# Sum of the experts' outputs: the second norm's scale and shift move from Pool to VectorE, in another order

## The chip, the cores and the metric

One NeuronCore of one Trainium2 chip runs the whole program, and the metric is the device time of one execution in microseconds. It has TensorE (PE), VectorE (DVE), ScalarE (ACT), GpSimd (POOL, here called Pool) and SyncE (SP), each with its own queue of instructions, which it works through in order.

## What is computed

Four blocks follow each other on x of 2 x 2048 x 256 (4096 rows of 256): agent attention, attention with a mixture of experts (MoE), a selective scan, and a feed-forward block with FP4 rounding. Each is wrapped as `x = x + layernorm(block(layernorm(x)))`. The change lies at the end of the second block, where the experts' outputs come together:

```python
    out = jnp.einsum('ne,end->nd', w, y)          # y = h @ W2 + b2, w: the two best gates
    ...
    x = _ln(src + attn_out, ln1_g, ln1_b)
    ff = _moe(x, gW, gb, W1, b1, W2, b2)
    return _ln(x + ff, ln2_g, ln2_b)
...
x = x + _layernorm(_L0_ffn_ref(_layernorm(x, axis=-1), ...), axis=-1)
x = x + _layernorm(_L1_attn_ref(_layernorm(x, axis=-1), ...), axis=-1)
```

`_L1_attn_ref` begins with a norm of its own with `w_norm` and `b_norm`.

## The kernel before, in words

`build` (end of the file) calls the stages one after another. Each stage opens its own buffers and semaphores and ends with a barrier of all engines. The change is in `moe_output`, which runs between `experts` and `scan_inputs`.

`moe_output` works on 8 groups (`GROUPS`) of 512 rows, each as 4 tiles (`GT`) of 128 rows by 256 channels. Every large buffer has two slots, for even and odd groups. For a group g the work goes like this:

- **Pool** gathers the two experts' output rows of every token from DRAM, by index, with eight indirect DMAs (`gather`, line 1661) into `back`.
- **TensorE** adds it all up in PSUM, in `ps_b[slot]` (`bias`, lines 1729 to 1733): b2 by gates, the row x of the norm before, and the two gathered rows. The text calls this pass g. `turn_gates` (line 1718) turns the gates for it, and ScalarE copies them (`copy_gate_t`, line 1670).
- **VectorE** takes the statistics of ps_b (`stats_y`, line 1605), and **ScalarE** norms it into y (`norm_y`, line 145).
- **Pool** multiplies y by ln2_g (line 1650) and adds ln2_b, giving v (line 1654), in `scale_y`. That is the second norm.
- VectorE takes the statistics of v (`stats_v`), ScalarE norms v in place (`norm_v`), VectorE adds x1 (`add_x1`, line 1632) giving x2 and takes its statistics; ScalarE norms x2 into xm (`norm_x2`), VectorE takes its statistics (`stats_xm`), ScalarE norms xm into xn (`norm_xm`), TensorE turns xn (`turn_xn`, line 1741), and ScalarE scales and shifts the turned xn and stores it (`scale_xn`, line 1703). SP loads x1 and stores x2 and xm.

So there are four norms in a row. The order of each engine's queue is written out by `run_stages`: in step s it issues every stage `(stage, behind)` for group s - behind, in the order of the list. With `unroll=True` all steps stand one after another. The arithmetic of all four norms' scales is done once a step for four groups at a time, each at another norm: `all_scales` on VectorE (lines 98 to 107, then, after ScalarE's line 113 and 115, lines 134 to 140). There are 11 such steps (`STEPS`, 0 to 10). In the text, step s begins on VectorE where line 98 of `all_scales(s)` starts.

The lists of the kernel before:

```python
dve:  (stats_y, 0), (stats_v, 1), (all_scales, 0, STEPS), (add_x1, 1), (stats_xm, 2)
pool: (gather, -2), (scale_y, 0)
act:  (copy_gate_t, -1), (all_rstd, 0, STEPS), (norm_y, 0), (norm_v, 1), (norm_x2, 2), (norm_xm, 3), (scale_xn, 4)
pe:   (turn_gates, -1), (bias, -1), (turn_xn, 4)
sp:   (load_x1, 0), (store_x2, 1), (store_xm, 2)
```

Waits that matter around the change: `gather(g)` waits for pass g-2 (`bias_ready`), whose rows lie in the same slot; pass g waits for its gathers, its copied gates and `norm_y(g-2)`; `scale_y(g)` waits for all four tiles of y; `add_x1(g)` waits for `norm_v(g)`, which ScalarE does in step g+1. Pool's queue starts with a wait for `loaded`, the five small loads that SP issues at the stage's start (b2, ln2_g, ln2_b, w_norm, b_norm), lines 1572 to 1577.

Of the kernel before, what the change touches and what calls it, by code (L numbers as in the profile page):

```python
# [16 lines left out]
ALU = mybir.AluOpType  # L17
# [3 lines left out]
P = 128  # L21
B, L, C = 2, 2048, 256
# [3 lines left out]
GT = 4  # L26
GN = GT * P
GROUPS = T // GN
# [102 lines left out]
def ln_scale(dve, chain, s, n, rstd_ready, scale_ready):  # L131

    dve.wait_ge(rstd_ready, n + 1)
    chain.then(dve.tensor_tensor(s.t[:, 0, :], s.r0[:, :], s.r0[:, :], ALU.mult))
    chain.wait()
    chain.then(dve.scalar_tensor_tensor(s.t[:, 0, :], s.t[:, 0, :], -0.5, s.var[:, :], ALU.mult, ALU.mult))
    chain.wait()
    chain.then(dve.scalar_tensor_tensor(s.rstd[:, :], s.t[:, 0, :], 1.5, s.r0[:, :], ALU.add, ALU.mult))
    chain.wait()
    dve.scalar_tensor_tensor(s.nmr[:, :], s.mean[:, :], -1.0, s.rstd[:, :], ALU.mult, ALU.mult).then_inc(scale_ready, 1)  # L140
# [12 lines left out]
def run_stages(eng, units, *stages, unroll=False, ways=2):  # L153

    stages = [(stage, behind, own[0] if own else units) for stage, behind, *own in stages]

    def step(s, way):
        for stage, behind, count in stages:  # L160
            if not isinstance(s, int) or 0 <= s - behind < count:
                stage(s - behind, (way - behind) % ways)

    starts, ends = [behind for _, behind, _ in stages], [behind + count for _, behind, count in stages]
    if unroll:
        for s in range(min(starts), max(ends)):
            step(s, s % ways)
        return

    first, last = -(-max(starts) // ways) * ways, min(ends) // ways * ways  # L170
    for s in range(min(starts), first):
        step(s, s % ways)
    with eng.Fori(first // ways, last // ways) as i:
        for way in range(ways):
            step(i * ways + way, way)
    for s in range(last, max(ends)):
        step(s, s % ways)


def third_on(unit):  # L180

    return not isinstance(unit, int) or unit >= 2
# [6 lines left out]
def over(ap, shape):  # L189

    return ap.broadcast_to(shape)
# [484 lines left out]
STEPS = NQ * QC  # L676
# [862 lines left out]
def moe_output(nc, io, scratch, route, sent, ident):  # L1539
# [3 lines left out]
    with ExitStack() as ctx:  # L1543
        r = Room(nc, ctx, "mo")
        NORMS = 4
        STEPS = GROUPS + NORMS - 1
        b2 = r.sb("b2", [E, C])
        rows = {n: r.sb(n, [P, 1, C]) for n in ("ln2_g", "ln2_b")}
# [4 lines left out]
        x1, y, v, x2, xm, xn = (r.sb(n, [P, 2, GT, C]) for n in ("x1", "y", "v", "x2", "xm", "xn"))  # L1553
# [5 lines left out]
        loaded = r.sem("loaded")  # L1559
# [4 lines left out]
        y_normed, y_scaled, v_ready, v_normed = (r.sem(n) for n in ("y_normed", "y_scaled", "v_ready", "v_normed"))  # L1564
        x2_ready, xm_ready, xn_normed = (r.sem(n) for n in ("x2_ready", "xm_ready", "xn_normed"))
# [3 lines left out]
        with nc.Block() as block:  # L1569
            @block.sync  # L1570
            def _(sp):
                sp.dma_start(b2[:, :], io["b2"]).then_inc(loaded, 16)
                for n, dst in rows.items():
                    sp.dma_start(dst[:, 0, :], over(io[n], [P, C])).then_inc(loaded, 16)
                with nc.allow_non_contiguous_dma("scale and shift by channel"):
                    for n, dst in columns.items():
                        sp.dma_start(dst[:, :], io[n].rearrange("o (k p) -> p (o k)", p=P)).then_inc(loaded, 16)

                def load_x1(g, slot):
                    if third_on(g):  # L1580
                        sp.wait_ge(x2_ready, g - 1)
                    sp.dma_start(x1[:, slot, :, :], rows_at(scratch.x1, g * GN)).then_inc(x1_loaded[slot], 16)

                def store_x2(g, slot):
                    sp.wait_ge(x2_ready, g + 1)
                    sp.dma_start(rows_at(scratch.x2, g * GN), x2[:, slot, :, :]).then_inc(x2_stored[slot], 16)

                def store_xm(g, slot):
                    sp.wait_ge(xm_ready, (g + 1) * GT)
                    sp.dma_start(rows_at(scratch.xm, g * GN), xm[:, slot, :, :]).then_inc(xm_stored[slot], 16)  # L1590

                for slot in range(2):

                    for s in (x2_stored, xm_stored, xn_t_stored):
                        sp.sem_inc(s[slot], 16)
                run_stages(sp, GROUPS, (load_x1, 0), (store_x2, 1), (store_xm, 2))
                for slot in range(2):
                    for s in (x2_stored, xm_stored, xn_t_stored):
                        sp.wait_ge(s[slot], (GROUPS // 2 + 1) * 16)

            @block.vector
            def _(dve):
                def stats(n, x):
                    for k in range(GT):
                        dve.bn_stats(ln.st[:, n * GT + k, :], x[:, k, :]).then_inc(stats_ready[n], 1)

                def stats_y(g, slot):
                    dve.wait_ge(bias_ready, g + 1)
                    stats(0, ps_b[slot])

                def stats_v(g, slot):
                    dve.wait_ge(v_ready, g + 1)
                    stats(1, v[:, slot, :, :])

                def all_scales(s, parity):
                    for n in range(NORMS):
                        if 0 <= s - n < GROUPS:
                            dve.wait_ge(stats_ready[n], (s - n + 1) * GT)
                    if s >= NORMS:
                        dve.wait_ge(xn_normed, (s - NORMS + 1) * GT)  # L1620
                    c = Chain(dve, steps, s * (VAR_STEPS + SCALE_STEPS))
                    ln_var(dve, c, ln, var_ready)
                    ln_scale(dve, c, ln, s, rstd_ready, scale_ready)
                    assert c.n == VAR_STEPS + SCALE_STEPS, c.n

                def add_x1(g, slot):
                    dve.wait_ge(x1_loaded[slot], (g // 2 + 1) * 16)
                    dve.wait_ge(x2_stored[slot], (g // 2 + 1) * 16)
                    dve.wait_ge(v_normed, (g + 1) * GT)
                    if g >= 2:  # L1630
                        dve.wait_ge(xm_ready, (g - 1) * GT)
                    dve.tensor_tensor(x2[:, slot, :, :], v[:, slot, :, :], x1[:, slot, :, :], ALU.add).then_inc(x2_ready, 1)
                    dve.wait_ge(x2_ready, g + 1)
                    stats(2, x2[:, slot, :, :])

                def stats_xm(g, slot):
                    dve.wait_ge(xm_ready, (g + 1) * GT)
                    stats(3, xm[:, slot, :, :])

                dve.memset(ln.st[:, :, :], 0.0).then_inc(stats_zeroed, 1)  # L1640
                dve.wait_ge(stats_zeroed, 1)
                run_stages(dve, GROUPS, (stats_y, 0), (stats_v, 1), (all_scales, 0, STEPS), (add_x1, 1), (stats_xm, 2), unroll=True)

            @block.gpsimd
            def _(pool):
                pool.wait_ge(loaded, 5 * 16)

                def scale_y(g, slot):
                    pool.wait_ge(y_normed, (g + 1) * GT)
                    pool.tensor_tensor(y[:, slot, :, :], y[:, slot, :, :], over(rows["ln2_g"][:, :, :], [P, GT, C]), ALU.mult).then_inc(y_scaled, 1)  # L1650
                    if third_on(g):
                        pool.wait_ge(x2_ready, g - 1)
                    pool.wait_ge(y_scaled, g + 1)
                    pool.tensor_tensor(v[:, slot, :, :], y[:, slot, :, :], over(rows["ln2_b"][:, :, :], [P, GT, C]), ALU.add).then_inc(v_ready, 1)

                def gather(g, slot):
                    if third_on(g):
                        pool.wait_ge(bias_ready, g - 1)
                    for a in range(2):
                        for t in range(GT):  # L1660
                            pool.indirect_dma_start(back[:, slot, a, t, :], None, scratch.sorted_y[:, :],  # L1661
                                                    bass.IndirectOffsetOnAxis(route.packed[:, a, g * GT + t:g * GT + t + 1], 0)).then_inc(gathered[slot], 16)

                run_stages(pool, GROUPS, (gather, -2), (scale_y, 0), unroll=True)

            @block.scalar
            def _(act):
# [1282 lines left out]
```

## Time and profile before

| | |
|---|---|
| median of 3 runs | 3812.51 us (3805.7 to 3818.8) |
| the profiled execution's own time | 3818.61 us |
| its span, first to last instruction | 3816.9 us |
| busy over the span | PE 86%, DVE 77%, ACT 54%, POOL 31% |
| mean granted clock of TensorE | 0.915 |
| stage `moe_output` in the span | 2146 to 2335 us |

The profile is of one execution, with times from the span's start. A row of the timeline is: start in us, length in us, engine, line, operation, output<-inputs, shape, count, and in brackets the idle time of that engine just before and what ended it. "issue" is time in which an engine waited for nothing that the profile shows. PEclk is the share of full speed that TensorE's clock was granted. PEld is TensorE's weight load.

### The profile page before, as it was taken

What the parts mean: (1) busy time and instruction counts of PE and PEld (TensorE: products, weight loads), DVE (VectorE), ACT (ScalarE), POOL (GpSimd) and SP (SyncE); (2) the same over time, 40 slices, a digit from 0 to 9 for tenths busy, and PEclk for the clock granted to TensorE, in tenths of its full rate; (3) what the DMA queues carried; (4) which work ended last, traced back from release to release, by engine and by line L of the source; (5) the groups of instructions that cost most, each with busy time, mean ns of one, the idle gap of its engine ahead of it and who ended that gap; (6) DMA issues with size and microseconds to landing.
All of it is one profiled execution on the core that took longest, in us unless ns stands there. A gap on an engine that the chain in (4) does not pass through costs nothing. (4 is left out here: it accounts for less than half of the span.)

```text
span 3816.9 us, 87664 instructions
## 1 busy us (share of the span) xinstructions
PE 3298.5 (86%) x34938; PEld 1884.3 (49%) x34939; DVE 2927.6 (77%) x4552; ACT 2057.6 (54%) x2972; POOL 1173.3 (31%) x910
## 2 busy tenths in 40 slices
PE   4769999999999999968699775997799999747876
PEld 1433333333333333326466552343687787546665
DVE  5659999998999999706344254676699999868986
ACT  0316777776777777833011155665565766334553
POOL 0100000000000000005100270000799999747775
PEclk8868999998999999967899866998899999879998
DMA  1674023030303120043222253333543434211110
GB/s 55 220 187 47 13 42 46 8 48 6 48 4 49 20 34 5 5 154 118 79 65 64 75 160 117 112 124 133 138 132 116 133 116 134 90 57 50 55 33 17
DMA packets 221875, 296.93 MB, mean 78 GB/s; under 512 B 56377, under 2 KB 154946, under 8 KB 219842
## 3 DMA queue, kind: packets, MB, share of 16 engines
q1 hardware_dynamic: 204258, 258.24, 25.1%
q0 software_dynamic: 6144, 17.05, 1.4%
q10 hardware_dynamic: 11120, 16.62, 1.3%
q8 instruction: 260, 4.26, 0.5%
q14 instruction: 93, 0.76, 0.1%
HBM read 174.75 MB, written 116.47 MB: 76 GB/s over the span
## 5 line engine op out<-in xcount | busy, mean ns | idle before, releaser
L921 DVE TENSOR_REDUCE att_maxima<-att_ps_m 128x1 f32<-128x512 f32 x2048 | 1286.4, 684 | 90.8 <-PE att_ps_m L977 89.3
L876 ACT ACTIVATE att_probs<-att_ps_s 128x1024 f32<-128x1024 f32 x1024 | 1000.0, 1022 | 289.9 <-PE att_ps_o L1004 276.7
L1004 PE MATMUL att_ps_o<-att_probs,att_vs 128*32 128x256 f32 x8192 | 662.6, 396 | 4.8 <-ACT att_probs L876 0.6
L977 PE MATMUL att_ps_m<-att_ks,att_qs 48*128 48x512 f32 x2048 | 587.3, 515 | 29.3 <-DMA att_ks<-scratch_k 28.6
L2235 POOL TENSOR_TENSOR ss_ch<-ss_h,ss_c_rep 128x1024 f32<-128x1024 f32 x256 | 601.6, 2416 | 12.4 <-DVE ss_h L2322 12.4
L2354 PE MATMUL ss_ps_u<-ss_diag,ss_dx_t 128*32 128x128 f32 x16384 | 476.0, 275 | 28.1 <-DMA ss_dx_t<-scratch_dx_t 14.6
L2354 PEld LDWEIGHTS ss_ps_u<-ss_diag,ss_dx_t 128*32 128x32 f32 x16384 | 454.2, 111 | 84.8 <-issue 63.9
L977 PEld LDWEIGHTS att_ps_m<-att_ks,att_qs 48*128 48x128 f32 x2048 | 238.7, 189 | 477.0 <-DVE att_maxima L921 393.6
L992 PE MATMUL att_ps_s<-att_qs,att_ks 50*128 50x512 f32 x2048 | 456.7, 407 | 4.0 <-DMA att_qs<-att_m_parts 1.2
L2274 ACT ACTIVATE ss_decay<-ss_delta,ss_a_neg 128x1024 f32<-128x1024 f32 x256 | 293.9, 1148 | 232.1 <-DVE ss_h L2322 210.1
L1004 PEld LDWEIGHTS att_ps_o<-att_probs,att_vs 128*32 128x32 f32 x8192 | 163.0, 108 | 365.1 <-issue 342.3
L2322 DVE TENSOR_TENSOR_SCAN ss_h<-ss_decay,ss_ps_u 128x1024 f32<-128x1024 f32 x128 | 286.4, 2275 | 47.5 <-PE ss_ps_u L2354 38.3
L2322 DVE TENSOR_TENSOR_SCAN ss_h<-ss_decay,ss_carry,ss_ps_u 128x1024 f32<-128x1024 f32 x128 | 293.2, 2334 | 7.7 <-POOL ss_ch L2235 4.8
L992 PEld LDWEIGHTS att_ps_s<-att_qs,att_ks 50*128 50x128 f32 x2048 | 223.4, 190 | 25.0 <-ACT att_probs L876 20.8
L856 POOL TENSOR_TENSOR att_heads<-att_o_t,att_sums 128x256 f32<-128x256 f32 x32 | 19.9, 621 | 702.0 <-DVE att_sums L936 702.0
L849 POOL TENSOR_TENSOR att_m_parts<-att_m_t,att_m_parts 16x128 fp32r<-16x128 f32 x32 | 14.4, 449 | 682.8 <-ACT att_m_parts L896 682.8
L1457 ACT ACTIVATE ex_y<-ex_ps_y,ex_x 128x256 f32<-128x256 f32 x72 | 34.1, 474 | 301.7 <-PE ex_ps_y L1528 301.7
L1661 POOL DMA_INDIRECT mo_back<-scratch_sorted_y,moe_packed x64 | 61.2, 956 | 345.5 <-DMA mo_b_norm<-in_b_norm 318.8
L2036 PE MATMUL si_ps_xz<-si_xn_t,si_w_in 128*128 128x512 f32 x256 | 119.4, 622 | 35.1 <-ACT si_xp L1984 15.8
L2375 PE MATMUL ss_ps_y<-ss_ch,ss_sum_block 128*32 128x512 f32 x1024 | 124.7, 602 | 15.3 <-POOL ss_ch L2235 15.1
L1510 PE MATMUL ex_ps_h<-moe_w_w,ex_x_t 128*128 x288 | 137.2, 599 | 0.4 <-issue 0.4
L1528 PE MATMUL ex_ps_y<-moe_w_w,ex_hid_t 128*128 x576 | 136.1, 379 | 0.0
(391 smaller groups left out, 4472.6 us busy)
## 6 DMA issues: line engine op xcount, KB each, us to landing
ss_delta<-scratch_delta SPq DMA_DIRECT2D x256, 128.0 KB, 3.1
att_qs<-scratch_q SPq DMA_DIRECT2D x96, 128.0 KB, 9.3
att_ks<-scratch_k SPq DMA_DIRECT2D x96, 128.0 KB, 10.7
ex_x<-scratch_sorted_x SPq DMA_DIRECT2D x72, 132.0 KB, 2.1
scratch_sorted_y<-ex_y SPq DMA_DIRECT2D x72, 128.0 KB, 1.7
scratch_v<-qkv_v_ext SPq DMA_DIRECT2D x8, 1024.0 KB, 4.4
scratch_q<-qkv_parts SPq DMA_DIRECT2D x16, 512.0 KB, 5.3
scratch_k<-qkv_parts SPq DMA_DIRECT2D x16, 512.0 KB, 6.0
```

The source lines that it names most:

```text
L876: act.activation(probs[:, (2 * n + pair) % 4, :, :], ps_s[pair][:, :, :], ACT.Exp, scale=HD ** -0.5).then_inc(exp_done, 1)
L921: dve.tensor_reduce(maxima[:, j, at:at + 1], ps_m[plan.bank(key)][:, :], AX.X, ALU.max).then_inc(maxed, 1)
L977: pe.matmul(ps_m[plan.bank(key)][:, :], qs[own, s // QC % 2, s % QC, p, t * P:(t + 1) * P], ks[own, s // QC % 2, p, c * GN:(c + 1) * GN], ...
L992: mm = pe.matmul(ps_s[pair][:, e, :], ks[rows_of(e, 0, ROWS), st // QC % 2, pair, kt * P:(kt + 1) * P], qs[rows_of(e, 0, ROWS), st // QC % ...
L1004: mm = pe.matmul(ps_o[h * VW:(h + 1) * VW, cols], vs[st // QC % 2][:, kt, h * VW:(h + 1) * VW], probs[:, (2 * n + h // 2) % 4, h % 2, cols ...
L1510: mm = pe.matmul(ps_h[slot][:, :], x_t[:, slot, k, :], w1[:, bass.ds(e, 1), k, :].rearrange("p a f -> p (a f)"), start=k == 0, stop=k == K ...
L1528: mm = pe.matmul(ps_y[slot][:, 0, :], hid_t[:, slot, f, :], w2[:, bass.ds(e, 1), f, :].rearrange("p a c -> p (a c)"), start=f == 0, stop=f ...
L2235: pool.tensor_tensor(ch[:, w.n % (CH_GROUPS * DQ), :], h[:, w.n % H_SLOTS, :], c_rep[:, w.ng, :], ALU.mult).then_inc(s["ch_ready"], 1)
L2274: act.activation(decay[:, w.n % DECAYS, :], delta[:, w.delta % DELTAS, :], ACT.Exp, scale=a_neg[:, at:at + 1]).then_inc(s["decay_ready"], 1)
L2322: dve.tensor_tensor_scan(h[:, w.n % H_SLOTS, :], decay[:, w.n % DECAYS, :], ps_u[w.n % U_BANKS][:, :], start, ALU.mult, ALU.add).then_inc( ...
L2354: mm = pe.matmul(ps_u[w.n % U_BANKS][q * DSUB:(q + 1) * DSUB, j * P:(j + 1) * P], dx_t[:, w.part % 2, j, w.dq * DSUB:(w.dq + 1) * DSUB], d ...
L2375: mm = pe.matmul(ps_y[dq * DSUB:(dq + 1) * DSUB, cols], block[:, :], ch[:, group % CH_GROUPS * DQ + dq, cols], start=False, stop=group % N ...
```

## The change

VectorE gets `scale_y`, with both operations as they were on Pool, and the wait for the five loads. Its list gets a new order, in which `all_scales` comes first in a step and `stats_y` works for the next group. Pool keeps only `gather`, with no wait for the loads and no waits for VectorE. The wait for x2 inside `scale_y` is dropped, since VectorE itself makes x2. The other engines' lists stay.

```diff
+                def scale_y(g, slot):
+                    dve.wait_ge(y_normed, (g + 1) * GT)
+                    dve.tensor_tensor(y[:, slot, :, :], y[:, slot, :, :], over(rows["ln2_g"][:, :, :], [P, GT, C]), ALU.mult).then_inc(y_scaled, 1)
+                    dve.wait_ge(y_scaled, g + 1)
+                    dve.tensor_tensor(v[:, slot, :, :], y[:, slot, :, :], over(rows["ln2_b"][:, :, :], [P, GT, C]), ALU.add).then_inc(v_ready, 1)
...
-                run_stages(dve, GROUPS, (stats_y, 0), (stats_v, 1), (all_scales, 0, STEPS), (add_x1, 1), (stats_xm, 2), unroll=True)
+                dve.wait_ge(loaded, 5 * 16)
+                run_stages(dve, GROUPS, (all_scales, 0, STEPS), (stats_y, -1), (scale_y, 0), (add_x1, 1), (stats_v, 0), (stats_xm, 2), unroll=True)
...
-                pool.wait_ge(loaded, 5 * 16)
-
-                def scale_y(g, slot):
-                    pool.wait_ge(y_normed, (g + 1) * GT)
-                    pool.tensor_tensor(y[:, slot, :, :], y[:, slot, :, :], over(rows["ln2_g"][:, :, :], [P, GT, C]), ALU.mult).then_inc(y_scaled, 1)
-                    if third_on(g):
-                        pool.wait_ge(x2_ready, g - 1)
-                    pool.wait_ge(y_scaled, g + 1)
-                    pool.tensor_tensor(v[:, slot, :, :], y[:, slot, :, :], over(rows["ln2_b"][:, :, :], [P, GT, C]), ALU.add).then_inc(v_ready, 1)
...
-                run_stages(pool, GROUPS, (gather, -2), (scale_y, 0), unroll=True)
+                run_stages(pool, GROUPS, (gather, -2), unroll=True)
```

VectorE, the end of step 2 of `moe_output` (from the last line of `all_scales(2)` to the first of `all_scales(3)`), as a difference. The names: mo_ps_b is the sum in PSUM, mo_x the buffers x1, x2, mo_ln_g and mo_ln_b the rows ln2_g and ln2_b.

```order
 L140 SCALAR_TENSOR_TENSOR mo_ln_nmr<-mo_ln_mean,mo_ln_rstd 128x16
-L1632 TENSOR_TENSOR mo_x<-mo_v,mo_x 128x1024
+L1605 BN_STATS mo_ln_stats<-mo_ps_b 128x6 x4
+L1613 TENSOR_TENSOR mo_y<-mo_y,mo_ln_g 128x1024
+L1615 TENSOR_TENSOR mo_v<-mo_y,mo_ln_b 128x1024
+L1638 TENSOR_TENSOR mo_x<-mo_v,mo_x 128x1024
 L1605 BN_STATS mo_ln_stats<-mo_x 128x6 x4
+L1605 BN_STATS mo_ln_stats<-mo_v 128x6 x4
 L1605 BN_STATS mo_ln_stats<-mo_xm 128x6 x4
-L1605 BN_STATS mo_ln_stats<-mo_ps_b 128x6 x4
-L1605 BN_STATS mo_ln_stats<-mo_v 128x6 x4
 L98 TENSOR_TENSOR mo_ln_t<-mo_ln_stats 128x16
```

The statistics of the next sum moved from the end of the step to right behind the arithmetic, ahead of the two operations that are new on VectorE and of the addition of x1.

Pool, the start of the stage before:

```order
L1644 UNCONDITIONAL_BRANCH
L1661 DMA mo_back<-scratch_sorted_y,moe_packed 128x256 x24
L1650 TENSOR_TENSOR mo_y<-mo_y,mo_ln_g 128x1024
L1654 TENSOR_TENSOR mo_v<-mo_y,mo_ln_b 128x1024
L1661 DMA mo_back<-scratch_sorted_y,moe_packed 128x256 x8
L1650 TENSOR_TENSOR mo_y<-mo_y,mo_ln_g 128x1024
```

And Pool's whole stage now:

```order
L1124 UNCONDITIONAL_BRANCH
L59 ISA x2
L1651 UNCONDITIONAL_BRANCH
L1658 DMA mo_back<-scratch_sorted_y,moe_packed 128x256 x64
L1569 UNCONDITIONAL_BRANCH
L59 ISA
```

The 64 gathers follow each other with nothing between them but their own waits for the passes.

## Rows read from the trace of the kernel before

**Rows 1.** Windows: busy us of each engine (instructions), PEclk, DMA share, GB/s.
```profile
2146.00:2335.00 189.00, 117.39 (x416) 78.29 (x416) 79.53 (x258) 83.08 (x174) 102.81 (x80) 0.64 0.43 135
...
2163.00:2179.00 16.00, 16.00 (x42) 10.26 (x43) 0.00 (x0) 0.00 (x0) 6.20 (x7) 0.50 0.23 66
...
2225.20:2233.60 8.40, 8.40 (x40) 5.73 (x41) 3.49 (x17) 4.94 (x12) 6.46 (x7) 1.00 0.36 103
2237.40:2247.40 10.00, 9.97 (x40) 6.86 (x41) 6.88 (x27) 2.72 (x7) 8.03 (x8) 0.83 0.71 225
2255.40:2271.30 15.90, 15.87 (x40) 10.33 (x41) 10.82 (x29) 8.25 (x18) 12.93 (x10) 0.50 0.67 209
```

**Rows 2.** Timeline of VectorE in the stage.
```profile
2146.21 0.14 DVE L1640 MEMSET mo_ln_stats<- 128x96 f32 x1 [6.50 <-PEq L60]
...
2180.52 0.19 DVE L98 TENSOR_TENSOR mo_ln_t<-mo_ln_stats 128x16 f32<-128x16 f32 x1
...
2201.76 1.23 DVE L1632 TENSOR_TENSOR mo_x<-mo_v,mo_x 128x1024 f32<-128x1024 f32 x1 [4.05 <-ACT mo_v L145]
...
2226.61 0.19 DVE L98 TENSOR_TENSOR mo_ln_t<-mo_ln_stats 128x16 f32<-128x16 f32 x1
...
2242.71 0.19 DVE L98 TENSOR_TENSOR mo_ln_t<-mo_ln_stats 128x16 f32<-128x16 f32 x1
...
2244.90 0.17 DVE L140 SCALAR_TENSOR_TENSOR mo_ln_nmr<-mo_ln_mean,mo_ln_rstd 128x16 f32<-128x16 f32 x1
2249.19 3.64 DVE L1632 TENSOR_TENSOR mo_x<-mo_v,mo_x 128x1024 f32<-128x1024 f32 x1 [4.12 <-ACT mo_v L145]
2252.86 1.41 DVE L1605 BATCH_NORM_STATS2 mo_ln_stats<-mo_x 128x6 f32<-128x256 f32 x4
2254.19 1.39 DVE L1605 BATCH_NORM_STATS2 mo_ln_stats<-mo_xm 128x6 f32<-128x256 f32 x4
...
2294.12 0.19 DVE L98 TENSOR_TENSOR mo_ln_t<-mo_ln_stats 128x16 f32<-128x16 f32 x1
...
2305.98 0.19 DVE L98 TENSOR_TENSOR mo_ln_t<-mo_ln_stats 128x16 f32<-128x16 f32 x1
```

**Rows 3.** Timeline of Pool in the stage.
```profile
2151.24 1.00 POOL L1661 DMA_INDIRECT mo_back<-scratch_sorted_y,moe_packed  x1 [318.79 <-DMA mo_b_norm<-in_b_norm]
...
2202.70 1.10 POOL L1661 DMA_INDIRECT mo_back<-scratch_sorted_y,moe_packed  x1 [0.30 <-issue]
...
2249.39 2.35 POOL L1650 TENSOR_TENSOR mo_y<-mo_y,mo_ln_g 128x1024 f32<-128x1024 f32 x1
2251.88 3.15 POOL L1654 TENSOR_TENSOR mo_v<-mo_y,mo_ln_b 128x1024 f32<-128x1024 f32 x1
```

**Rows 4.** Groups of Pool in the stage: busy us, mean ns, idle before.
```profile
L1661 POOL DMA_INDIRECT mo_back<-scratch_sorted_y,moe_packed x64 | 61.2, 956 | 345.5 <-DMA mo_b_norm<-in_b_norm 318.8 <-issue 17.5 <-PE mo_ps_b L1733 8.7
L1654 POOL TENSOR_TENSOR mo_v<-mo_y,mo_ln_b 128x1024 f32<-128x1024 f32 x8 | 22.8, 2848 | 1.0
L1650 POOL TENSOR_TENSOR mo_y<-mo_y,mo_ln_g 128x1024 f32<-128x1024 f32 x8 | 18.8, 2352 | 22.3 <-ACT mo_y L145 22.2
```

**Rows 5.** Timeline of TensorE: first matmuls of passes 1, 3, 6 and 7.
```profile
2180.48 0.69 PE L1729 MATMUL mo_ps_b<-mo_b,mo_gate_t 8*128 8x256 f32 x2 [0.68 <-ACT mo_gate_t L1670]
...
2207.68 1.19 PE L1729 MATMUL mo_ps_b<-mo_b,mo_gate_t 8*128 8x256 f32 x2 [7.80 <-DMA mo_back<-scratch_sorted_y,moe_packed]
...
2255.43 1.22 PE L1729 MATMUL mo_ps_b<-mo_b,mo_gate_t 8*128 8x256 f32 x2 [6.51 <-ACT mo_gate_t L1670]
...
2275.30 1.09 PE L1729 MATMUL mo_ps_b<-mo_b,mo_gate_t 8*128 8x256 f32 x2 [2.14 <-ACT mo_gate_t L1670]
```

**Rows 6.** Timeline of ScalarE: a full step, its first and last row.
```profile
2245.11 1.94 ACT L145 ACTIVATE mo_y<-mo_ps_b,mo_ln_nmr,mo_ln_rstd 128x256 f32<-128x256 f32 x4 [0.94 <-DVE mo_ln_nmr L140]
...
2254.80 0.59 ACT L1670 ACTIVATE mo_gate_t<-mo_ps_g 8x512 f32<-8x512 f32 x1 [0.54 <-ACT mo_xn_t L1703]
```

**Rows 7.** Line 592, an earlier stage, a row repeated as second input: min/median/max ns.
```profile
L592 DVE TENSOR_TENSOR qkv_x<-x_x,x_agent_ln x8: 1215/1790/2023, 106.6 to 195.7; 128x1024 f32 x6, 128x1024 f32<-128x1024 f32 x2
```

## The prediction

> **What bounds the kernel now.** The time is a sum of stages one after another, with barriers between them, so I first look for the stage that the edit touches. The busy row of the stage (first of [rows 1]) puts it at 2146 to 2335 us, 189 us of 3816.9, and says that Pool is the busiest compute engine beside TensorE, and that TensorE's clock was granted at 0.64 of full speed there. Nothing outside this stretch is edited, so only its length can move. Next I read the stage as a timeline, one engine at a time.
>
> VectorE [rows 2]: each step starts its short arithmetic at line 98. Step 0 starts it at 2180.52, step 7 at 2294.12, step 8 at 2305.98, which is 113.6 us for seven steps (16.2 each). From line 98 to the end of line 140 take 2.4 us. Then VectorE idles 4.1 us until ScalarE has normed v, and adds x1.
>
> Pool [rows 3]: in steps 3 to 5 it has no idle time to speak of. Eight gathers at 1.25 us from start to start (956 ns and 0.30 of issue, 10.0 in all, [rows 3, 4]), a multiplication (2.35) and an addition (3.15) are with their gaps one turn of 15.6 us. VectorE's steps, 16.2 on average, are little longer. The two are coupled: VectorE's addition at 2249.19 takes 3.64 us beside Pool's multiplication at 2249.39, and the one at 2201.76 takes 1.23 where Pool only gathers [rows 2, 3].
>
> TensorE [rows 1, 5]: one pass of eight (lines 1729 to 1733 for a group) lasts 8.4 us at a granted clock of 1.0 (2.4 GHz) and 15.9 at 0.5 (1.2 GHz). Groups 0 and 6 are at the low clock, 4 at the high one, 5 in between (0.83, 10 us). Of the windows left out, groups 3 and 7 read 0.50 and 0.51, and groups 1 and 2 are high. After 7.8 and 6.5 us without a matmul a pass began at the low clock (2207.68 and 2255.43, [rows 5]); group 7 did too after 2.1 us. After 0.7 us (group 1) it was high.
>
> ScalarE [rows 6]: a full step is 10.3 us, from the first row of y (2245.11) to the end of the gate copy (2254.80 + 0.59), and only then does the next-but-one pass start (2255.43, [rows 5]).
>
> **The change, part by part.**
>
> *Pool's wait on the loads goes.* Pool's first gather starts at 2151.24, when the last of five loads has landed [rows 3]; VectorE's first instruction of the stage is at 2146.21 [rows 2]. Without the wait Pool begins at about 2146.4, so gathers 0 and 1 come 4.8 us earlier, and pass 0 starts at 2158.1 instead of 2162.88 (its gates, which do wait for the loads, are ready before that). Worth **-4.8 us** at the front. VectorE takes the wait over at no cost: it has nothing to do before 2179.
>
> *Pool loses 16 operations.* 22.8 + 18.8 = 41.6 us of busy time [rows 4]. Its turn falls from 15.6 to 10.0 us, so it no longer bounds. What is late next is the question.
>
> *VectorE gains 16 operations.* The price of one, 128x1024 with both inputs in SBUF: 1.22 us is the lowest in this kernel for a repeated row as second input (1215 ns, [rows 7]), 1.23 for the addition beside gathers [rows 2]. The upper end is 2.02 (2023 ns). I take 1.26 with its gap, since no Pool arithmetic is left to meet. 16 x 1.26 = 20 us. They lie behind the next group's `stats_y` in VectorE's queue.
>
> *The new order.* After the arithmetic of step s VectorE now waits for TensorE's pass s+1, and behind that wait stand `scale_y(s)`, `add_x1(s-1)`, `stats_v(s)` and `stats_xm(s-2)`, together 2 x 1.26 + 1.26 + 3 x 1.33 = 7.8 us (four statistics are 1.33 us from start to start, 2252.86 to 2254.19, [rows 2]), or 9.1 with `stats_y` itself. Before, behind a late pass stood only `stats_y` and `stats_v` (2.7 us). So the loop through ScalarE and TensorE gets longer: arithmetic 2.4, ScalarE's step 10.3, pass 8.4 or 15.9, signals 0.2, VectorE 9.2, which is 30.5 or 38.0 us for two steps, 15.3 or 19.0 a step. The same loop before: 2.4 + 10.3 + 8.4 or 15.9 + 0.3 + 2.8, 12.1 or 15.9 a step. **Pool's 15.6 us turn is swapped for a loop of 15.3 to 19.0**. Against that, steps 0 to 3 have a short ScalarE step (norms of 1.9 us each, 1.94 in [rows 6], one, two, three and four of them), so there the loop is shorter.
>
> *The sum, step by step.* I replayed the eight steps with these durations: a pass starts when its gates are copied (ScalarE done with the step before the last, one copy of 0.6) and its gathers have landed (10.0 us after the first plus 1.9 to 3.9; I take 2.9; the last gather of group 3, 2202.70 + 1.10, let pass 3 start at 2207.68, [rows 3, 5]; those of group g+2 begin when pass g ends). From pass 6 on, the turning of xn, its scaling and the copy come between, 4.0 us in all (2271.3 to 2275.30, [rows 1, 5]). I give each pass the clock that a like idleness ahead of it got in [rows 5]. Passes start at: 0 at 2158.1 (low), 1 at 2175.8 (high, 1.8 us after pass 0), 2 at 2186.2 (high), 3 at 2197.4 (high: 2.8 us after pass 2, in which the next gates are turned, where it was 7.8 of pure idleness), 4 at 2211.7 (low: it now waits 5.9 us for ScalarE's step 2), 5 at 2229.4 (high), 6 at 2250.0 (low, 12 us after pass 5), 7 at 2269.9 (low, as before). Line 98 then starts at 2175.6, 2189.7, 2202.7, 2215.2, 2237.0, 2249.3, 2275.3 and 2295.2, and at 2307.5 for step 8. The trace of before has 2294.12 and 2305.98 for the last two [rows 2]. So the kernel runs 11 us ahead at step 3 (2226.61 before, [rows 2]), and has lost all of it by step 6. Steps 9 and 10 have nothing moved. **Sum: +1.5 us.**
>
> *Against the median.* The profiled execution took 3818.61 us, with a span of 3816.9; the median of the three runs is 3812.51, and they spread from 3805.7 to 3818.8. The sum is a difference, so I put it on the median: 3812.5 + 1.5 = **3814 us**. The profiled execution itself would become 3820.
>
> **A rule weighed.** Where they meet, Pool's addition takes 3.15 us against 2.35 for its multiplication of the same size, and VectorE's addition 3.64 against 1.23 [rows 2, 3]. The Trainium skill, page "SBUF — State Buffer", section "Who interferes with whom", says that a VectorE instruction with two SBUF inputs shares a read interface with GpSimd instructions that read SBUF, and that whoever comes first holds it for the whole instruction. The trace agrees: VectorE's 3.64 us end 1.1 us after Pool's multiplication does. By that rule alone the change would gain 2.4 us in each of three steps. In my sum this gain is not on the path, because VectorE waits for the pass anyway.
>
> **The rivals.**
>
> *A, faster: TensorE stays at the high clock once warm.* Pool's relief closes the 7.8 us hole before pass 3, and each pass at the high clock is 7.5 us shorter than at the low one. With pass 0 low and all others high the same replay puts step 8 at 2287.1, 19 us earlier: 3793.6. For it: less idleness in the first half. Against it: 6 to 8 us holes before passes 4, 5, 6 and 7 remain in that replay, and holes of 6.5 and 7.8 us gave the low clock [rows 5]. Chance 0.14; with pass 7 alone at the high clock it is -6 us, still within my range.
>
> *B, slower: VectorE's queue held behind low-clock passes.* If passes 1 to 7 all run at 0.5, each step is 15.9 us plus the 1.8 to 4.0 us between passes, 17.7 to 19.9, and step 8 comes at 2325.0: +19.0, 3831.5. It decides from the sixth low pass on: with passes 0 and 3 to 7 low it is +5.2, with all low +19. For it: group 7 was low 2.1 us behind the work ahead of it [rows 5], and passes 4 to 7 have longer waits in my replay. Against it: the pass that followed within 0.7 us was high, and the first three after pass 0 follow closely. Chance 0.17.
>
> *C, slower: VectorE's arithmetic and Pool's gathers hold each other up.* Three additions a step now fall among gathers. If each waited for a gather of 1.00 us, it would be 3 x 1.00 x 7 = 21 us: 3833. Against it stands the addition at 2201.76, which took its 1.23 us although a gather began inside it, at 2202.70; that gather took 1.10 instead of the 1.00 of the first [rows 2, 3]. 0.1 to 0.2 us on Pool is hidden in a turn of 10 us. Chance 0.03.
>
> *D: the edit does not bring the early start,* since something else holds Pool until 2151. Then pass 0 is where it was, and up to 4.8 us come on top of the sum: 3819, inside the range. Chance 0.04.
>
> **How the numbers follow.** A measurement of this kernel can tell 0.3%, 11.4 us, from no change. My forecast, with its variants of one pass more or less at the high clock (-6 to +5) and D, lies within 0.3%: 0.63 in all, 0.59 for the forecast and 0.04 for D. Faster by over 0.3%: A and mixes near it, 0.17. Slower by over 0.3%: B and C, 0.20. The range reaches from 3800, two thirds of the way to A, to 3829, close to B; the price of VectorE's operation at its upper end (2.02 for 1.26, some 0.8 x 2 a step, 11 us at most) lies within it.
>
> **What would show it right or wrong.** Right: Pool's first gather near 2146.5; gathers never again behind arithmetic; VectorE's three additions at 1.2 to 1.3 us each; VectorE's idle time falling mostly ahead of `stats_y`, named "PE mo_ps_b", with none left on "POOL mo_v"; line 98 of step 3 about 11 us earlier and of step 7 level with before. Wrong: if VectorE idles ahead of `scale_y` or `add_x1` instead; if passes 4 and 6 run at clock 1.0 (rival A); if additions take 2 us (C). The claim that the new order gives back what Pool's relief brings would be wrong if step 7 came over 10 us earlier at the same clocks.

## The result, and the profile after

The changed kernel takes 3821.29 us in the median of 18 runs (3807.18 to 3834.38); the kernel before, measured beside it, takes 3807.57 us (3801.28 to 3824.95, 18 runs). The ratio is 1.0035, with a 95% interval of 1.0022 to 1.0048: slower by 13 us, where I had forecast 1.5 us more. The time lies inside the range (3800 to 3829). It is a small loss, just past the 0.3% that can be told from no change, and so it falls in the class that the prediction gave 0.20.

The profile has to be read with care here, and the reason is the main lesson of this case. The profiled execution of the changed kernel took 3807.18 us, the least of its 18 runs; the profiled one of the kernel before took 3818.61, well above its median. So the two profiles alone would say that the change gains 11 us. What goes with the time from run to run is TensorE's granted clock. The runs list its mean over the whole span, and within each kernel a run with 0.001 less takes about 3.4 us more (the slope within the 10 kernels timed here, 191 runs). As far as the profiles show, most of that happens in stages that the edit does not touch; see the table behind experiments 10 and 11. In the 18 runs of the changed kernel the extremes are 0.920 at 3807.18 and 0.912 at 3834.38.

The stage in the first profile of the changed kernel, by windows with the columns of [rows 1]:

```profile
2144.00:2319.00 175.00, 102.25 (x416) 68.67 (x416) 89.81 (x274) 81.96 (x173) 65.39 (x64) 0.71 0.45 143
```

It answers to the first row of [rows 1]: Pool is down from 102.8 to 65.4 us, VectorE up from 79.5 to 89.8, and the clock was 0.71, not 0.64. Next Pool, as a timeline; the first row and a stretch of step 1:

```profile
2144.78 0.99 POOL L1658 DMA_INDIRECT mo_back<-scratch_sorted_y,moe_packed  x1 [316.46 <-POOLq L60]
...
2193.16 0.95 POOL L1658 DMA_INDIRECT mo_back<-scratch_sorted_y,moe_packed  x1 [1.52 <-PE mo_ps_b L1730]
2194.41 1.89 POOL L1658 DMA_INDIRECT mo_back<-scratch_sorted_y,moe_packed  x1 [0.30 <-issue]
2196.60 0.95 POOL L1658 DMA_INDIRECT mo_back<-scratch_sorted_y,moe_packed  x1 [0.30 <-issue]
```

The stage's first VectorE instruction is at 2144.12, so Pool starts 0.66 us after it, where it started 5.0 us after it before [rows 2, 3]. Pool now idles until a pass has freed its slot, here for 1.52 us. TensorE waits for gathers only ahead of pass 0, where before it also waited 7.80 us for them ahead of pass 3 [rows 5].

VectorE through one whole step, step 4, with the start of step 5:

```profile
2229.40 0.19 DVE L98 TENSOR_TENSOR mo_ln_t<-mo_ln_stats 128x16 f32<-128x16 f32 x1 [0.23 <-issue]
...
2232.82 0.17 DVE L140 SCALAR_TENSOR_TENSOR mo_ln_nmr<-mo_ln_mean,mo_ln_rstd 128x16 f32<-128x16 f32 x1
2240.56 1.43 DVE L1605 BATCH_NORM_STATS2 mo_ln_stats<-mo_ps_b 128x6 f32<-128x256 f32 x4 [7.56 <-PE mo_ps_b L1730]
2241.90 1.21 DVE L1613 TENSOR_TENSOR mo_y<-mo_y,mo_ln_g 128x1024 f32<-128x1024 f32 x1
2243.15 1.23 DVE L1615 TENSOR_TENSOR mo_v<-mo_y,mo_ln_b 128x1024 f32<-128x1024 f32 x1
2244.29 1.22 DVE L1638 TENSOR_TENSOR mo_x<-mo_v,mo_x 128x1024 f32<-128x1024 f32 x1
2245.54 1.41 DVE L1605 BATCH_NORM_STATS2 mo_ln_stats<-mo_x 128x6 f32<-128x256 f32 x4
2246.86 1.40 DVE L1605 BATCH_NORM_STATS2 mo_ln_stats<-mo_v 128x6 f32<-128x256 f32 x4
2248.17 1.40 DVE L1605 BATCH_NORM_STATS2 mo_ln_stats<-mo_xm 128x6 f32<-128x256 f32 x4
2249.79 0.19 DVE L98 TENSOR_TENSOR mo_ln_t<-mo_ln_stats 128x16 f32<-128x16 f32 x1 [0.23 <-issue]
```

ScalarE has normed the rows y about 2 us after the step's scales are done (2232.99), and v 2 us later. VectorE could then work on them, but its queue has `stats_y` of the next group in front, and that waits 7.56 us for TensorE. The 9.2 us from 2240.56 to 2249.79 are what I had put behind the pass. What TensorE did meanwhile:

```profile
2227.88 1.22 PE L1726 MATMUL mo_ps_b<-mo_b,mo_gate_t 8*128 8x256 f32 x2 [9.35 <-issue]
2231.88 1.22 PE L1726 MATMUL mo_ps_b<-mo_b,mo_gate_t 8*128 8x256 f32 x2
2235.89 1.00 PE L1726 MATMUL mo_ps_b<-mo_b,mo_gate_t 8*128 8x256 f32 x2
2238.32 0.69 PE L1726 MATMUL mo_ps_b<-mo_b,mo_gate_t 8*128 8x256 f32 x2
...
2244.00 0.69 PE L1726 MATMUL mo_ps_b<-mo_b,mo_gate_t 8*128 8x256 f32 x2 [2.17 <-ACT mo_gate_t L1667]
```

Pass 5 begins after 9.35 us without a matmul, at the low clock: its second and third tile start 4.0 us after the one before. The fourth starts 2.4 us after the third, so the clock has risen meanwhile. Step 5 then has a short wait, and step 6 follows:

```profile
2252.94 1.43 DVE L1605 BATCH_NORM_STATS2 mo_ln_stats<-mo_ps_b 128x6 f32<-128x256 f32 x4 [0.85 <-PE mo_ps_b L1730]
...
2262.17 0.18 DVE L98 TENSOR_TENSOR mo_ln_t<-mo_ln_stats 128x16 f32<-128x16 f32 x1 [0.23 <-DVE mo_ln_stats L1605]
```

Two steps, from line 98 at 2229.40 to line 98 at 2262.17, are one turn of the loop (arithmetic of step 4, ScalarE, pass 6 at the high clock, VectorE in step 5): 32.8 us, 30.5 in my sum.

Who waited for whom, VectorE in the stage, before and now (us in total, times, longest). Before:

```profile
DVE mo_ln_stats L1605 <- PE mo_ps_b L1733: 48.9, 5, 32.7
DVE mo_x L1632 <- ACT mo_v L145: 31.0, 8, 4.1
DVE mo_ln_stats L1605 <- POOL mo_v L1654: 6.1, 2, 3.2
```

The changed kernel:

```profile
DVE mo_ln_stats L1605 <- PE mo_ps_b L1730: 51.5, 6, 24.9
DVE mo_ln_stats L1605 <- DMA scratch_x<-qkv_x: 7.8, 1, 7.8
DVE mo_x L1638 <- ACT mo_v L145: 2.3, 1, 2.3
```

The waits on ScalarE fell from 31.0 to 2.3 us and those on Pool (6.1) are gone, as intended. Those on TensorE grew from 48.9 to 59.3 us, although 8 us of the start's wait went (32.7 to 24.9). I count the 7.8 us into them: the transfer that the row names is one of an earlier stage, and the instruction is again `stats_y`.

### The profile page after: what moved, and what is told of

Its sections match the earlier page's. It is cut to its first block and busy times, and to the rows that moved or that the text cites. A ratio compares the mean times of both kernels' runs of the same rounds, so it can differ in the third digit from the quotient of the medians.

```text
span 3805.4 us, 87658 instructions
## 1 busy us (share of the span) xinstructions
PE 3272.7 (86%) x34938; PEld 1877.3 (49%) x34939; DVE 2934.7 (77%) x4568; ACT 2059.7 (54%) x2972; POOL 1136.2 (30%) x894
## 5 line engine op out<-in xcount | busy, mean ns | idle before, releaser
L2232 POOL TENSOR_TENSOR ss_ch<-ss_h,ss_c_rep 128x1024 f32<-128x1024 f32 x256 | 602.2, 2440 | 10.2 <-DVE ss_h L2319 10.2
L2351 PE MATMUL ss_ps_u<-ss_diag,ss_dx_t 128*32 128x128 f32 x16384 | 477.1, 275 | 28.7 <-DMA ss_dx_t<-scratch_dx_t 14.3
L1658 POOL DMA_INDIRECT mo_back<-scratch_sorted_y,moe_packed x64 | 65.4, 1022 | 357.8 <-POOLq L60 316.5
```

Source lines behind the costliest of these rows:

```text
L2232: pool.tensor_tensor(ch[:, w.n % (CH_GROUPS * DQ), :], h[:, w.n % H_SLOTS, :], c_rep[:, w.ng, :], ALU.mult).then_inc(s["ch_ready"], 1)
L2351: mm = pe.matmul(ps_u[w.n % U_BANKS][q * DSUB:(q + 1) * DSUB, j * P:(j + 1) * P], dx_t[:, w.part % 2, j, w.dq * DSUB:(w.dq + 1) * DSUB], d ...
```

## The experiments

Two theories stood at first. **Q**: VectorE's queue stands behind TensorE's next pass, so late and low-clock passes cost more than before. **V**: VectorE's 16 new operations cost the time. A third, **O**, put the loss outside the stage. Kernels timed together on one chip share the runs of the kernel before.

**1. The changed kernel once more.**

> The changed kernel once more, for a second profile and for times beside the variants on the same chip. Theory Q (queue and clock: VectorE's queue stands behind the next pass, so a pass at the low clock costs more than before): slower than the kernel before by 5 to 18 us in the median, and this profile shows more passes of TensorE at the low clock than the first profile of it (which had a pass time of 85 us summed over eight groups), with the stage as much longer as the passes. Theory O (something outside the stage, such as another stage's start or the longer VectorE program, costs the time): the stage is again shorter than before by 5 us or more and the loss stands elsewhere in the span.

Measured: 3818.44 us in 12 runs, beside 3806.12 for the kernel before in 35. Ratio 1.0036 [1.0018, 1.0053]. The loss is real and repeats. The mean clock of the runs is 0.9159 against 0.9181. But this profile again caught a short execution, 3811.99 us, with a stage of 175 us, 9 us shorter than before. So what theory Q expected of the time came, and what it expected of the profile did not: of the stage, what theory O expected came.

**2. VectorE's work in the old order.**

```diff
-                run_stages(dve, GROUPS, (all_scales, 0, STEPS), (stats_y, -1), (scale_y, 0), (add_x1, 1), (stats_v, 0), (stats_xm, 2), unroll=True)
+                run_stages(dve, GROUPS, (stats_y, 0), (stats_v, 1), (all_scales, 0, STEPS), (scale_y, 0), (add_x1, 1), (stats_xm, 2), unroll=True)
```

> scale_y is on VectorE and Pool only gathers, without the wait for the loads, but VectorE keeps the order of before, with scale_y put ahead of add_x1. Theory Q: Pool's relief and the early start are kept and nothing stands behind a late pass that was not there before, so it is faster than the kernel before by 8 to 15 us. Theory V (VectorE's 16 operations themselves, 20 us, or their meeting with the gathers, cost the time): it is as slow as the changed kernel, 10 us or more above the kernel before.

Measured: 3799.0 us, ratio 0.9977 [0.9962, 0.9993]. The same 16 operations on VectorE, the same relief of Pool, and it is 7 us faster than before and 19 us faster than the changed kernel. V falls. So does O as a matter of the longer program, since this one is as long. The gain is smaller than the 8 to 15 us expected. And it need not come from Pool's relief: experiment 8 has the early start alone and a ratio of 0.9985, which these intervals do not tell from 0.9977.

**3. One stage moved to the end of the step.**

```diff
-                run_stages(dve, GROUPS, (all_scales, 0, STEPS), (stats_y, -1), (scale_y, 0), (add_x1, 1), (stats_v, 0), (stats_xm, 2), unroll=True)
+                run_stages(dve, GROUPS, (all_scales, 0, STEPS), (scale_y, 0), (add_x1, 1), (stats_v, 0), (stats_xm, 2), (stats_y, -1), unroll=True)
```

> The changed kernel with one stage moved: stats_y of the next group stands at the end of the step, behind scale_y, add_x1, stats_v and stats_xm, where it was second. Theory Q: 15 to 25 us faster than the changed kernel, and 8 to 16 us faster than the kernel before, about as old_order_dve. Theory V: no better than the changed kernel.

Measured: 3799.26 us, ratio 0.9981 [0.9964, 0.9998], 19 us below the changed kernel on the same chip, as expected (15 to 25), though only 7 us below the kernel before (8 to 16 expected). This is the sharpest of the tests, since nothing but the place of `stats_y` in VectorE's queue differs. The stage in its profile is 160 us, against 172 to 175 in the four of the changed kernel.

**4. The new order alone, Pool as before.**

```diff
-                run_stages(dve, GROUPS, (stats_y, 0), (stats_v, 1), (all_scales, 0, STEPS), (add_x1, 1), (stats_xm, 2), unroll=True)
+                run_stages(dve, GROUPS, (all_scales, 0, STEPS), (stats_y, -1), (add_x1, 1), (stats_v, 0), (stats_xm, 2), unroll=True)
```

> The new order on VectorE alone; Pool keeps scale_y and the wait for the loads. Theory Q: the new order costs without Pool's relief to pay for it, about 10 us slower than the kernel before (5 to 15), with Pool's turn of 15.6 us still in the way. Theory V: as the kernel before, since VectorE has none of the 16 operations.

Measured: 3815.0 us, ratio 1.0018 [1.0002, 1.0034]: slower by some 7 to 9 us without any of the 16 operations. That agrees with Q. (The edit moves `stats_v` and `all_scales` too, not `stats_y` alone.) VectorE's wait for passes is 64.8 us there:

```profile
DVE mo_ln_stats L1605 <- PE mo_ps_b L1733: 64.8, 6, 27.5
DVE mo_x L1632 <- ACT mo_v L145: 10.6, 4, 4.1
DVE mo_ln_stats L1605 <- POOL mo_v L1654: 5.6, 4, 3.2
```

**5 to 7. TensorE kept busy.** The next three ask how much of it is the clock; their two theories, K and L, stand in the text for warm_before. Behind the turning of each group's gates, TensorE does four matmuls more, into a bank that nobody reads:

```diff
+        ps_w = r.ps("ps_w", [P, GN])
...
                     mm.then_inc(gate_turned, 1)
+                    for _ in range(4):
+                        pe.matmul(ps_w[:, :], ident[:, :], route.xa_t[:, 0, :GN], start=True, stop=True)
```

> The kernel before with four extra matmuls (128x512, read by nobody) on TensorE behind each turning of the gates, 3.4 us at the high clock, to fill the holes between the passes. Theory K (the low clock in the holes decides what a late pass costs): passes at the low clock become fewer, and since Pool's turn of 15.6 us bounds this kernel anyway, it gains little: 0 to 7 us faster than the kernel before. Theory L (only the longer queue on VectorE counts, at any clock): unchanged or slower by what the extra matmuls delay, 0 to 5 us.

> The changed kernel with the same four matmuls. Theory K: its passes move to the high clock, and it comes within 5 us of warm_before, so it gains 8 to 15 us on the changed kernel. Theory L: it stays 10 us or more above warm_before, since the order of VectorE's queue is the same.

> sy_last with the same four matmuls: the version that might beat all. Theory K: 12 to 22 us faster than the kernel before, 5 to 15 faster than sy_last, as every pass after the first is at the high clock. Theory L: as sy_last, or slower by up to 5 us.

| | median us (runs) | ratio to the kernel before | mean clock of its runs |
|---|---|---|---|
| kernel before, same chip | 3811.91 (29) | | 0.9163 |
| warm_before | 3809.7 (12) | 0.9986 [0.9966, 1.0006] | 0.9213 |
| warm_after | 3812.14 (12) | 0.9984 [0.9967, 1.0000] | 0.9219 |
| warm_sy_last | 3786.13 (6) | 0.9921 [0.9895, 0.9946] | 0.9252 |

With the clock held higher in both, the changed kernel's loss is not seen: warm_after and warm_before have the same ratio. That is what theory K expected. The intervals are wide: a loss of 13 us would show in them, one of 5 us would not. The changed kernel had 1.0036 on its chip and warm_after has 0.9984 on its own, which is 12 us by the medians and 20 by the ratios (8 to 15 expected). The profiles speak less clearly: warm_before has one pass above 10.7 us (14.3), warm_after has two (12.7 and 14.8), and its stage is 7 us the longer (175.0 against 167.9). The place of `stats_y` counts here too: warm_sy_last is 26 us below warm_after, and 26 below the kernel before, more than the 12 to 22 expected. Its profile shows a stage where all passes take 8.6 us, and from step 2 to step 7 VectorE's steps are 13.3 us apart. VectorE, steps 3 to 5, from line 98 on:

```profile
2211.91 0.19 DVE L98 TENSOR_TENSOR mo_ln_t<-mo_ln_stats 128x16 f32<-128x16 f32 x1
...
2216.21 1.23 DVE L1614 TENSOR_TENSOR mo_y<-mo_y,mo_ln_g 128x1024 f32<-128x1024 f32 x1 [2.00 <-ACT mo_y L145]
2217.47 1.22 DVE L1616 TENSOR_TENSOR mo_v<-mo_y,mo_ln_b 128x1024 f32<-128x1024 f32 x1
...
2225.24 0.19 DVE L98 TENSOR_TENSOR mo_ln_t<-mo_ln_stats 128x16 f32<-128x16 f32 x1
...
2238.60 0.19 DVE L98 TENSOR_TENSOR mo_ln_t<-mo_ln_stats 128x16 f32<-128x16 f32 x1
```

There the multiplication waits 2.00 us for ScalarE's y and for nothing else; the statistics of the next pass are taken when the rest is done.

**8. The early start alone.**

```diff
-                pool.wait_ge(loaded, 5 * 16)
-
                 def scale_y(g, slot):
+                    if g == 0:
+                        pool.wait_ge(loaded, 5 * 16)
```

> The kernel before with one thing changed: Pool waits for the five loads ahead of its first multiplication, not ahead of its first gather. If the early start is worth what I put it at, it is 4.8 us faster than before (3 to 7). If the 4.8 us are given back in Pool's turn or by the clock, it is within 2 us of the kernel before.

Measured: 3803.24 us beside 3811.91, ratio 0.9985 [0.9963, 1.0007]. The ratio means 6 us and fits 4.8, but the interval takes in no change. In its profile pass 0 starts 12.4 us after the stage's start, in both profiles of the kernel before 16.7: the early start itself is 4.3 us. Yet the whole stage is 20 us shorter there than in those two profiles (163.5 against 183.9), as the passes sum to 86.8 us and not to 100. So one pair of profiles says 20 us where the runs say about 6.

**9. A second profile of the kernel before.**

> The kernel before once more, for a second profile of it. If the first profile of it caught a bad draw of the clock (passes summing to 100 us in a stage of 184 us, at 3818.6 us against a median near 3808), this one has passes of 85 to 95 us and a stage of 165 to 178 us. If the first was typical, the stage is again above 180 us.

**10 and 11. A third and a fourth profile of the changed kernel.**

> The changed kernel for a third profile. Its first two caught good draws (3807.2 and 3812.0 us against a median near 3820). Theory Q: where its time is near 3820, the passes sum to 95 us or more and the stage is above 180 us, and two low passes in a row put VectorE's step at 18 us or more. Theory O: the stage stays near 175 us whatever the time is.

> The changed kernel for a fourth profile, since the first three were draws with a high clock (3797.8 to 3812.0 us against a median near 3820), while both profiles of the kernel before were draws with a low one. Theory Q: if this execution is near 3820 us or above, its passes sum to 95 us or more and its stage lasts above 178 us; if it is near 3807, it looks like the first three (passes 85 to 93, stage 172 to 175). Theory O: the stage is near 175 us in either case.

The lengths of the passes and of the stage, read from the timelines of all six profiles (us). The stage is counted from VectorE's first instruction to the end of the last matmul, and the rest is the span less the stage:

| profile | time | passes 0 to 7 | sum | stage | rest |
|---|---|---|---|---|---|
| before | 3818.6 | 16.1, 8.6, 8.6, 16.1, 8.6, 10.2, 16.1, 16.0 | 100.1 | 183.9 | 3633.0 |
| before_again | 3820.8 | 16.1, 8.6, 8.6, 16.1, 8.6, 10.2, 16.1, 15.9 | 100.1 | 183.8 | 3635.2 |
| changed | 3807.2 | 12.5, 8.6, 10.2, 14.3, 8.6, 12.7, 8.6, 10.9 | 86.3 | 174.8 | 3630.6 |
| after_again | 3812.0 | 12.6, 8.6, 10.2, 8.6, 10.5, 16.1, 15.9, 10.2 | 92.8 | 175.1 | 3635.1 |
| after_third | 3797.8 | 10.7, 8.6, 8.6, 14.3, 8.6, 12.7, 8.6, 12.5 | 84.5 | 172.3 | 3623.8 |
| after_fourth | 3803.5 | 10.6, 8.6, 8.6, 14.3, 8.6, 12.7, 8.6, 12.5 | 84.5 | 172.2 | 3629.5 |

So the expectations on a profile near the changed kernel's median could not be tested. For before_again the second case came ("the first was typical": again above 180 us), but again in an execution above the median of its kernel. Both profiles of the kernel before have the same pattern to 0.1 us. All four of the changed kernel lie below its median, three of them below each of its 28 runs that were not profiled, so they are not a fair sample of it. On one more chip a single run of the kernel before took 3833.22 us beside after_fourth's 3803.47, the other way round from the medians.

The table says two things more. First, where the time varies: in the four profiles of the changed kernel it moves by 14 us, the stage by 3 and the rest by 11. Over all fourteen profiles of this case the rest goes from 3619.8 to 3647.4 us, as much as the runs spread. One of the stages in it is `attention_output`, which no edit here touches. Its windows in early_gather and in warm3_sy_last:

```profile
1643.40:1843.80 200.40, 124.76 (x563) 90.98 (x563) 72.93 (x300) 39.93 (x80) 65.47 (x93) 0.60 0.42 145
1646.30:1832.00 185.70, 114.08 (x563) 81.97 (x563) 72.41 (x300) 39.92 (x80) 65.58 (x93) 0.65 0.46 157
```

It is 14.7 us shorter at a granted clock of 0.65 than at 0.60. So a run's mean clock tells largely what other stages drew.

Second, no profile shows the loss: the stage is 9 to 12 us shorter in each of the four than in the two of the kernel before, and the rest is not longer. For the eight variants the median of the runs less the profile's stage is 3634 to 3642 us (3628 for warm3_sy_last). For the kernel before it is 3622 to 3631, and for the changed kernel 3643 to 3649. By this estimate the profiles of the kernel before show a stage some 10 us too long for it, and those of the changed kernel one some 8 us too short. That the loss lies elsewhere in the span is not excluded by a profile, only made unlikely by sy_last, whose edit is in this stage and takes 19 us back.

**12. The best version found, with three extra matmuls instead of four.**

> warm_sy_last with three extra matmuls instead of four. In warm_sy_last TensorE itself sets the step (8.6 pass, 3.4 extra, 1.4 turning: 13.4 us). With three, if every pass stays at the high clock, a step is 12.5 us and the kernel 4 to 7 us faster than warm_sy_last. If holes let the clock fall again, it is slower than warm_sy_last by 2 to 10 us.

Measured: 3778.75 us in 6 runs, ratio 0.9927 [0.9900, 0.9954]. In ratio that is the same as warm_sy_last (0.9921), so the 4 to 7 us more were not to be seen; its profile has passes 0 and 6 at 10.2 us, the others at 8.6, and from step 2 on the steps are still 13.3 to 13.5 us apart. With less work on TensorE the step stayed as long, so TensorE alone did not set it. Either version is 0.7 to 0.8% faster than the kernel before, some 28 us, and beats both kernels of this case.

## Why the prediction was right in its range, and off in its sum

**Pool's wait and the early start: right.** -4.8 us forecast; pass 0 starts at 12.4 us into the stage instead of 16.7, -4.3.

**Pool no longer bounds: right.** Its busy time fell by 37 us, and it waits for passes now.

**The price of VectorE's operations: right.** 1.14 to 1.25 us each from start to start, 1.26 forecast. That they lie behind the pass was right as well (9.2 us behind it, 9.2 forecast).

**The loop of 15.3 to 19.0 us a step: right in size.** 32.8 us for two steps with a pass at the high clock, 30.5 forecast. And it is the place of `stats_y` in it that costs: moving it to the step's end wins 19 us (sy_last), and the new order in the kernel before costs 7 to 9 (only_order).

**Line 98, step by step.** Forecast, from the stage's start: 29.4, 43.5, 56.5, 69.0, 90.8, 103.1, 129.1 and 149.0 us. The first profile has 26.5, 42.0, 56.6, 73.0, 85.3, 105.7, 118.1 and 138.4. The first steps agree within 4 us. The last two differ by 11 because passes 4 and 6 ran wholly, 0 and 7 partly at the high clock in that execution, where I had each of them low (3 and 5 went the other way). I had step 7 level with the kernel before. It came 9 to 12 us earlier in all four profiles (136 to 139 us, against 147.9), at other clocks than forecast. For the profiled execution I had forecast 3820 us, and it took 3807.

**The step that failed is the clock that I gave each pass**, "the clock that a like idleness ahead of it got in [rows 5]". I read it off one execution and took it for a rule. The four profiles of the changed kernel do not bear it out: pass 0 took 10.6 to 12.6 us where I had it low (15.9), pass 4 8.6 in three and 10.5 in the fourth where I had it low, and pass 3, which I had high, 14.3 in three of them. Three patterns were seen in four executions. Their passes sum to 84 to 93 us, those of the kernel before to 100. The sum set one fixed pattern of the kernel before (four low passes) against one of mine (four low passes) and came to +1.5, which neither the profiles (a stage 9 to 12 us shorter) nor the runs (13 us longer) show. That the time fell inside the range is partly luck: two unlike errors lie behind one number. Where the two ran side by side (after_again, 12 runs and 35), the mean clock was 0.9159 against 0.9181. At 3.4 us for 0.001 that would be 7.5 us of the 12.7 between their mean times, and the other 5 us would be there at equal clock. So what I had left out seems to be a shift of the average clock, and that the longer queue makes each late or low pass count for more. This division is argued from the means and seen in no profile. The mean covers the whole span, and a stage that is longer at the low clock lowers it by itself.

**The baseline.** I put the difference on the median of three runs, 3812.5. The later medians of the kernel before are 3807.6, 3806.1, 3811.9 and 3814.5. That moved the absolute time by less than the sum was off.

**The rivals.** B, "VectorE's queue held behind low-clock passes", had 0.17, and the measured +13 lies between its two prices of +5.2 and +19. Its queue is shown (sy_last, only_order). Its low-clock passes are not: no profile of the changed kernel has more than two passes wholly low. A did not happen in the timed runs, though the profiles went part of its way. C was wrong in its price, but something of it was there, on Pool and not on VectorE; see the last section. D was wrong.

**The rule on the shared port.** VectorE's additions of x1 now take 1.22 us throughout, where they took 3.64 to 4.07 beside Pool's multiplication: that the two hold each other up, as the Trainium skill says ("SBUF — State Buffer", section "Who interferes with whom"), is so here. That whoever comes first holds the interface for the whole instruction is not what the trace of before shows, and my "the trace agrees" was too much:

```profile
2233.18 4.07 DVE L1632 TENSOR_TENSOR mo_x<-mo_v,mo_x 128x1024 f32<-128x1024 f32 x1 [4.12 <-ACT mo_v L145]
2233.80 2.35 POOL L1650 TENSOR_TENSOR mo_y<-mo_y,mo_ln_g 128x1024 f32<-128x1024 f32 x1
```

VectorE's addition began first, by 0.62 us here and by 0.20 at 2249.19, and still ended 1.1 us after Pool's multiplication, which took its usual 2.35. I had put the gain from its going off the path; no run tests that alone.

**What stays open.** No profile caught an execution at its kernel's median, so which passes go low in the typical one, and how the 13 us divide over the steps, is not seen. That the place of `stats_y` costs 19 us is shown. How much of it comes through the clock is argued. What Pool's relief is worth by itself stays open too: the runs do not tell the early start alone (0.9985) from the early start with the relief (0.9977).

## What to carry to other kernels

In a queue that is worked in order, an instruction that waits for the slowest partner of the step belongs behind everything that is already possible: one stage moved from second to last place was worth 19 us here, and 26 with TensorE's clock held up. Work moved off the engine that bounds a stage can come to nothing, or to a loss, by the order in the queue that takes it. And where a granted clock or another draw moves the time by more than the effect looked for, a single profile before and after can show the wrong sign; list the passes of several executions, split each span into the edited stage and the rest, and go by the times of the runs.

## What the runs showed of the hardware that I had not expected

**A gather that begins inside a VectorE operation with two SBUF inputs is held up by it.** In the changed kernel the gather at 2194.41 takes 1.89 us where the others take 0.95, and VectorE's multiplication runs from 2194.27 for 1.21 us:

```profile
2194.27 1.21 DVE L1613 TENSOR_TENSOR mo_y<-mo_y,mo_ln_g 128x1024 f32<-128x1024 f32 x1
2195.51 1.22 DVE L1615 TENSOR_TENSOR mo_v<-mo_y,mo_ln_b 128x1024 f32<-128x1024 f32 x1
2196.65 1.22 DVE L1638 TENSOR_TENSOR mo_x<-mo_v,mo_x 128x1024 f32<-128x1024 f32 x1
```

It ends 0.82 us later than VectorE's multiplication does. The same is seen at 2209.49 (1.89) and 2242.05 (1.88). The gather that took 1.10 us in the kernel before, at 2202.70 [rows 3], began 0.29 us before such an operation ended, and it too ended 0.82 us behind it. VectorE's own operations keep their 1.21 to 1.23 us. It is about 0.93 us on Pool in five of the steps, and TensorE did not wait for these gathers. The "SBUF — State Buffer" page of the Trainium skill says in that same section that a `tensor_tensor` with two SBUF inputs contends only with GpSimd's reads. It infers that the making of a DMA's descriptors is not held up by it. Here the gather, which Pool issues and which reads its row numbers from SBUF (moe_packed), is held up. Whether it is this read that waits, no run shows.

**A few idle microseconds of TensorE can be worth filling with matmuls that nobody needs.** Four of 128x512 behind each turning of the gates, 3.5 us of TensorE at the high clock, took sy_last from 3799.26 to 3786.13 us on another chip. Against the kernel before on its own chip, that is from 7 us faster to 26 us faster. The mean granted clock of the whole span rose from 0.9181 to 0.9252. In the kernel before, the same four gained nothing that the runs could tell (0.9986 [0.9966, 1.0006]).
